# Two low parts per batch moved from GpSimd to VectorE in a decoder layer's cross-attention

## The reference

```python
x = x + attn(layernorm(x))                       # one head of 128, 256 keys
x = x + cross_attn(layernorm(x), ctx_768)        # 16 heads of 64, 1601 keys of width 96
x = x + ffn(layernorm(x))                        # router picks 31 rows a batch; attention
                                                 # among them, then a GELU MLP; others pass through
# the cross-attention, per head:
sim  = (x @ Wq)_h @ (context @ Wk)_h.T * 64 ** -0.5
out  = softmax(sim) @ (context @ Wv)_h ;  y = concat(out) @ Wo + bo
```

## Time and profile before

| | |
|---|---|
| median of 3 runs | 2159.55 us (2159.05 to 2160.88) |
| the profiled execution, its own time | 2161.14 us |
| its span, first to last instruction | 2159.90 us |
| granted TensorE clock over the span | 0.997 |
| busy: PE, DVE, ACT, POOL | 2078.4, 1723.5, 1796.4, 1936.6 us |

### The profile page before, as it was taken

The page is one execution under the profiler, slowest core; times in us unless marked ns, Lnnn a source line. Parts: engine busy times, 40 slices in busy tenths (PEclk is TensorE's granted clock), DMA queues, the critical chain, the costliest instruction groups (busy, mean ns, idle before and its releaser), DMA issues.

```text
span 2159.9 us, 57506 instructions
## 1 busy us (share of the span) xinstructions
PE 2078.4 (96%) x21697; PEld 1409.5 (65%) x21697; DVE 1723.5 (80%) x4158; ACT 1796.4 (83%) x3064; POOL 1936.6 (90%) x1129
## 2 busy tenths in 40 slices
PE   8999999999999999999999999999999999999998
PEld 4667666666766666666666666667666666666664
DVE  7778878787887878879687787887878788886864
ACT  5888898888888888898788888888888888888872
POOL 3899999999999899999899998998999999899991
PEclk9999999999999999999999999999999999999999
DMA  3211000010100001010010100101000010100000
GB/s 75 59 38 30 2 16 16 2 29 2 30 2 10 21 2 29 2 30 2 11 29 2 30 2 2 29 2 29 2 19 21 2 29 2 17 2 2 2 11 11
DMA packets 70483, 35.16 MB, mean 16 GB/s; under 512 B 58944, under 2 KB 68032, under 8 KB 70208
## 3 DMA queue, kind: packets, MB, share of 16 engines
q1 hardware_dynamic: 69104, 31.28, 6.2%
q10 hardware_dynamic: 1104, 0.20, 0.1%
HBM read 16.46 MB, written 2.10 MB: 9 GB/s over the span
## 4 chain that ended last, share of the span: by engine, by line
PE 73%; DVE 13%; issue 6%; ACT 5%; POOL 2%; DMA 0%; DVEq 0%; SPq 0%; ACTq 0%; POOLq 0%
PE PS L585 13%; PE PS L626 13%; PE PS L586 13%; PE PS L602 11%; PE PS L604 10%; DVE EH L1102 5%; PE PS L649 4%; PE PS L636 2%; DVE over L1128 2%; PE PS L659 2%; ACT PF L910 2%; POOL EL L1580 2%; ACT EH L917 1%; ACT over L932 1%; DVE junk L1373 1%
## 5 line engine op out<-in xcount | busy, mean ns | idle before, releaser
L1580 POOL TENSOR_TENSOR EL<-PF,EH 128x1024 f16<-128x1024 f32 x828 | 1761.7, 2154 | 132.6 <-DVE EH L1102 60.7
L910 ACT ACTIVATE PF<-PS 128x512 f32<-128x512 f32 x1664 | 973.4, 600 | 218.8 <-PE PS L586 203.2
L602 PE MATMUL PS<-Ch,EH 128*128 128x97 f16 (+1 forms) x6656 | 762.2, 207 | 35.6 <-POOL EL L1580 32.0
L602 PEld LDWEIGHTS PS<-Ch,EH 128*128 128x128 f16 (+1 forms) x6656 | 604.3, 97 | 283.2 <-issue 109.4
L1102 DVE TENSOR_SCALAR_CACHE_REDUCE EH<-PF 128x1024 f16<-128x1024 f32 x621 | 746.0, 1209 | 17.6 <-ACT PF L910 17.6
L604 PE MATMUL PS<-Cl,EL 128*128 128x97 f16 (+1 forms) x6656 | 758.9, 206 | 0.0
L1128 DVE CUSTOM_DVE_ANT_1 over<-over,PS 128x802 f32<-128x802 f32 x512 | 505.1, 987 | 289.7 <-PE PS L626 146.5
L604 PEld LDWEIGHTS PS<-Cl,EL 128*128 128x128 f16 (+1 forms) x6656 | 594.6, 98 | 155.0 <-issue 1.4
L585 PE MATMUL PS<-AH,ChT 98*128 98x512 f16 x1664 | 635.2, 382 | 8.9 <-ACT PF L910 6.2
L586 PE MATMUL PS<-AL,ClT 96*128 96x512 f16 x1664 | 632.9, 380 | 0.0
L932 ACT ACTIVATE over<-PS 128x802 f32<-128x802 f32 x512 | 431.3, 842 | 32.7 <-PE PS L626 12.3
(11 more groups left out here) (250 smaller groups left out, 1653.4 us busy)
## 6 DMA issues: line engine op xcount, KB each, us to landing
Cf<-in_ctx SPq DMA_DIRECT2D x16, 576.0 KB
X<-in_x SPq DMA_DIRECT2D x16, 128.0 KB, 2.5
out_x<-X SPq DMA_DIRECT2D x16, 128.0 KB, 1.7
msk<-in_attention_mask SPq DMA_DIRECT2D x4, 256.0 KB, 4.5
AH<-mh SPq DMA_DIRECT2D x63, 2.0 KB
xWqT<-in_xWqT SPq DMA_DIRECT2D x2, 256.0 KB, 5.9
xWo<-in_xWo SPq DMA_DIRECT2D x2, 256.0 KB, 3.8
fw<-in_fw SPq DMA_DIRECT2D x2, 256.0 KB, 3.1
```

The costliest lines, as they stand in the source:

```text
L602: pe.matmul(PS[:, 6, u0:u0 + DC + 1], EH[0:kr, r, qs], Ch[j][0:kr, t, 0:DC + 1], start=(t == 0 and q == 0), stop=False, skip_group_check=True)
L910: act.activation(PF[:, n % PRING, :], PS[0:KP, 4 + n % 2, :], ACT.Exp).then_inc(sg("ex"), 1)
L1580: pool.tensor_tensor(EL[:, r - 1:r + 1, :], PF[:, f - 1:f + 1, :], EH[:, r - 1:r + 1, :], ALU.subtract).then_inc(sg("lo_pool"), 1)
```

## The change

Pairs 8 and 36 of each batch (tiles 16 and 17, 72 and 73) get their low part from VectorE and not from GpSimd. For both, the high part is ScalarE's. The place in the order stays: VectorE makes it right behind its rounding of pair 9 or 37. Since the low parts of a batch now count on two semaphores in another pattern, `lowered` looks the counts up in two tables. `LAST_PAIRS` is 828, the first of the last four pairs.

```diff
--- before.py
+++ after.py
@@ -45,6 +45,7 @@
 AV_LAG = 8
 ROUND_LAG = 2
 LO_LAG = 4
+LOW_BY_DVE = (8, 36)
 NQ = 4
 NKEY = -(-NC // NQ)
 EARLY = 4
@@ -480,9 +481,18 @@
                 return sg("eh_act"), p - LAST_PAIRS + LAST_PAIRS // 4 + 1
             return (sg("eh_act"), p // 4 + 1) if p % 4 == 0 else (sg("eh_dve"), p // 4 * 3 + p % 4)
 
+        LOW_PAIRS = TILES // 2
+        def low_by_dve(p):
+
+            return p >= LAST_PAIRS or p % LOW_PAIRS in LOW_BY_DVE
+
+        dve_lows = [p for p in range(TOTAL // 2) if low_by_dve(p)]
+        dve_low_at = {p: x + 1 for x, p in enumerate(dve_lows)}
+        pool_low_at = {p: x + 1 for x, p in enumerate([p for p in range(TOTAL // 2) if p not in dve_low_at])}
+
         def lowered(p):
 
-            return (sg("lo_dve"), p - LAST_PAIRS + 1) if p >= LAST_PAIRS else (sg("lo_pool"), p + 1)
+            return (sg("lo_dve"), dve_low_at[p]) if p in dve_low_at else (sg("lo_pool"), pool_low_at[p])
 
         def bank_of(s):
 
@@ -1101,7 +1111,7 @@
                         w.wait_ge(sg("av"), n - ERING + 1)
                     dve.tensor_scalar(EH[:, r - 1:r + 1, :], PF[:, f - 1:f + 1, :], KEEP, None, ALU.mult, ALU.add,
                                       accum_out=esum[:, r // 2:r // 2 + 1]).then_inc(sg("eh_dve"), 1)
-                elif k == "lo" and s.a[0] >= LAST_PAIRS:
+                elif k == "lo" and low_by_dve(s.a[0]):
                     n = 2 * s.a[0] + 1
                     f, r = n % PRING, n % ERING
                     w.wait_ge(sg("ex"), n + 1)
@@ -1568,7 +1578,7 @@
                     which = int(k[-1])
                     w.wait_ge(sg(f"ln_mv{which}"), i)
                     rsqrt(rstd[:, which, :], mv[:, which, :, 1], T, 1.0, LN_EPS, f"ln_rstd{which}")
-                elif k == "lo" and s.a[0] < LAST_PAIRS:
+                elif k == "lo" and not low_by_dve(s.a[0]):
                     n = 2 * s.a[0] + 1
                     f, r = n % PRING, n % ERING
                     w.wait_ge(sg("ex"), n + 1)
```

## The result

The changed kernel takes 2182.10 us (median of 4, 2181.46 to 2184.00), the kernel before 2159.49 on the same chip (median of 4, 2159.05 to 2160.88): a ratio of 1.0105 (95% interval 1.0088 to 1.0123). It is 22.6 us slower, where 8.1 us were forecast. The profiled execution took 2184.0 us with a span of 2182.7 at a granted clock of 0.998. Lines of the program behind the change stand 10 lower than before: 636 is now 646, 1102 is 1112, 1580 is 1590.

A forecast was written before the change was run, and what follows sets the result against it. TensorE (96% busy) sets the pace mostly, chained to VectorE and GpSimd in paced stretches. Terms 2.6 + 2.0 + 2.85 + 1.75 - 1.1 = +8.1 us on the 2159.55 median gave 2167.7; case range 2164 to 2174, 8 in 10 2158 to 2177.

The forecast's parts named there:

- The prices: Moved low part on VectorE: 1.2 us at pair 36, 1.5 to 1.6 at pair 8; keys' difference 1.5 instead of 0.57.
- The term of pair 14: Pair 8's move makes pair 14 0.3 us late in batches 1 to 4, 6, 8, 10, 12, 14: +2.6 us.
- the step that failed: Pair 36: work queued behind the low part up to 1.14 us late; TensorE loses at pair 43 or the spread keys.
- The three terms: Pair 36's move: pair 43 late, batches 0, 2, 3, +2.0 us; 6, 10, 14, +2.85; spread keys, 5, 9, 13, +1.75.
- moves with them: Batches 6, 10, 14: pairs 40 to 43 move by 0.93 us and TensorE, waiting at pair 43, too: +2.85 us.
- In 5, 7, 9, 11, 13 and 15 GpSimd waits before pair 12 or 13 anyway and the lateness is gone: Pair 8's move: in these batches GpSimd's waiting absorbs the lateness, so no loss is counted.
- In batch 0 TensorE comes later: Pair 8's move: in batch 0 TensorE comes later, so no loss is counted.
- The low part gets the lock when pair 35 ends: Batch 15, pair 36: VectorE goes first after GpSimd's pair 35; GpSimd loses 1.09 of 2.14 us saved: -1.1 us.
- No difference: Rival: lateness is won back at following TensorE waits; within 0.2%, some 4.3 us, 2163.1 us; chance 0.2.
- Faster: Rival: keys' difference gets in ahead of pair 10, pair 14 0.4 us earlier in up to 12 batches; 2153 us; chance 0.12.
- much slower: Rival: GpSimd wins at pair 36, TensorE 1.9 us late in 14 batches, +27 us, 2187 us; chance 0.08.
- the forecast 9.2 before batch 15: Sum of the loss terms for pairs 8 and 36, 2.6 + 2.0 + 2.85 + 1.75 us, without batch 15's -1.1.

The follow-up runs named there:

- experiment 3: Against only pair 36's low part moved to VectorE: that low part put behind the projection's sum, 2195.91 us; or the sum put one place earlier, 2171.98 us.
- Experiment 2: Kernel before, no low part moved, plus a 1.22 us VectorE instruction with one SBUF input at pair 36's place: 2176.36 us, ratio 1.0070.
- experiment 5: Only pair 8 on VectorE, keys' difference two places later in VectorE's order: 2154.60 us; that shift alone in the kernel before: 2158.38 us.
- pair 28: Only pair 28's low part moved to VectorE, against the kernel before: 2148.45 us, ratio 0.9950.
- low part of pair 32: Only pair 32's low part moved to VectorE, against the kernel before: 2177.09 us, ratio 1.0093.
- the filler: Only pair 32's low part on VectorE, with an added VectorE instruction of some 0.7 us ahead of it: 2176.35 us, ratio 1.0076 against the kernel before.

## Why the prediction was wrong

**What held.** The work ends up slower by waits of VectorE's making; GpSimd's relief goes into its idle time (102.8 us waiting for roundings, 60.7 before), and the 1.98 us before pair 14 are still 1.98. GpSimd and TensorE at pair 14 of batch 3, with the earlier trace rows before:

```profile
473.19 4.23 POOL L1590 TENSOR_TENSOR EL<-PF,EH 128x1024 f16<-128x1024 f32 x2 [1.98 <-DVE EH L1112]
...
475.47 0.20 PE L612 MATMUL PS<-Ch,EH 128*128 128x97 f16 x1 [0.41 <-POOL EL L1590]
```

The prices held: 1.22 us at pair 36 (batches 0 to 14), 1.62 to 1.66 at pair 8 (forecast 1.5 to 1.6), line 1131 at a median of 1.535 (forecast 1.5). The term of pair 14, 9 x 0.29 = 2.6 us, was 2.9, though part of it shows at pair 10 already. One sign failed: GpSimd's busy time was to fall by about 64 us and fell by 42.8, because its low parts behind the moved ones carry their wait for VectorE as busy time. And one reading was slightly off: 469.02 less 468.88 is 0.14 and not 0.12, which changes no term. The trace agrees with the Trainium skill's page "SBUF — State Buffer", section "Who interferes with whom", that VectorE's two-input instructions and GpSimd's exclude each other.

**Pair 36, the step that failed.** "All that is queued behind it is late by up to 1.14: the projection's sum, the rounding of pair 38, a maximum, the queries' low part" is what happened. But I followed that lateness only through the roundings, to GpSimd and pair 43, and never asked who waits for the sum. TensorE does, 0.6 us later in the same place. Forecast for the place: +4.85 us at pair 43 and 1.75 at the spread keys; measured: 14.7 at pair 36, in all batches but the last, and nothing at pair 43, since TensorE then arrives there later itself. The three terms were real mechanisms hidden below a larger one, as experiment 3 shows; two had about the forecast size at their pair, but only 0.45 to 0.49 of 0.67 and 0.4 of 0.95 were kept, so "moves with them" held for less than half of that 0.95. The third has its size as a wait (0.60 against 0.58), to which TensorE's clock adds 1.7 to 3.4 us when the wait is that long. Experiment 2 shows the 1.03 to be a matter of the queue alone.

**Pair 8, "In 5, 7, 9, 11, 13 and 15 GpSimd waits before pair 12 or 13 anyway and the lateness is gone".** This again follows GpSimd only. The keys' difference, forecast rightly to be 1.0 late, has VX or XA right behind it in those five batches, and TensorE's projection waits for them: 4.8 us. "In batch 0 TensorE comes later" was wrong too: the rounding of pair 9 makes TensorE wait 0.41 us more at pair 8 (the same in experiment 5), and the clock fell behind it for 1.55, which may be chance. Together 6.8 us where 0 stood.

**Batch 15, "The low part gets the lock when pair 35 ends", -1.1 us.** VectorE did not get it. Its low part there took 4.85 us, behind a normalization and pair 37 of GpSimd:

```profile
2105.74 4.85 DVE L1120 TENSOR_TENSOR EL<-PF,EH 128x1024 f16<-128x1024 f32 x1
```

TensorE lost 1.1 us at pair 36 and had 0.7 back at pair 37. The table's -0.8 for that batch is what is left of this loss, less the fall of the clock that only the execution before had there.

**The rivals.** "No difference" assumed that lateness is won back; in batches 0 to 14 TensorE won back none of what it lost at pairs 9 and 36. "Faster" and "much slower" both exist, 0.4 us at pair 14 and 1.9 at pair 36, one step of VectorE's order away from the change; in the change itself neither happened. The sum of the terms seen at their places, 14.7 + 4.8 + 2.9 + 2.0 = 24.4 us, takes the place of the forecast 9.2 before batch 15.

## What to carry to other kernels

When work is put into an engine's queue, go through every instruction that is queued behind it up to that engine's next idle time, and for each ask who waits for it: also for the small ones that only free a PSUM bank. An average load says nothing here: GpSimd was at 90% and VectorE at 80%, and the same 1.22 us in VectorE's queue cost 1.0 us a batch at pair 36 and gained 0.9 at pair 28. And of two engines that exclude each other, an instruction that now meets the other is longer itself and makes all behind it late; put it where nothing urgent is behind it, as the keys' difference in experiment 5.

## What the runs showed of the hardware

A VectorE instruction with two SBUF inputs that waits for the shared port isn't always next when GpSimd's instruction ends. If GpSimd's following instruction is ready, either may go first, and a lost meeting costs one more GpSimd instruction, 2.1 us:

| GpSimd in a low part, its next one a low part | VectorE asked before GpSimd's end, us | the next one's rounding was ready before that end, us | lost |
|---|---|---|---|
| low part of pair 8, five kernels | 0.54 to 0.58 | 0.46 to 0.51 | 0 of 75 |
| first half of a split, batches 5 to 14, 14 kernels | 0.86 to 0.88 | 0.79 to 0.80 | 0 of 140 |
| the same, batches 1 to 4 | 0.95 to 1.00 | 0.87 to 0.92 | 11 of 56 |
| low part of pair 32, batches 1 to 14 | 1.14 to 1.17 | 1.07 to 1.10 | 12 of 14 |
| the same with the filler ahead of it | 0.54 to 0.55 | 1.07 to 1.10 | 9 of 14 |

The Trainium skill ("SBUF — State Buffer", "Who interferes with whom") says that issue order decides who blocks. By that VectorE, which asked 0.5 to 1.2 us before GpSimd could have started its next instruction, would win all five; the trace agrees for the first two rows, nearly always for the third, and disagrees for the others.

What decides stays open. It isn't the time that VectorE has asked, since 0.54 never lost in the first row and lost nine times in the last. The third column orders the rows: the longer GpSimd's next low part had been ready, the more meetings VectorE lost, and the filler, which did not change that time, helped little. This was read from the traces only; no run changed that time alone. It can't be the whole rule either: the second halves of 185 splits, asked 0.75 us before the end of a low part with a normalization next that had been ready for 1.9 us, all went first.

The other surprise is the clock. A wait of TensorE of 1.81 to 1.84 us for the spread keys was followed by a granted clock of 0.50 in five of six cases (batches 5, 9 and 13 in both kernels of experiment 3), one of 1.21 to 1.24 us at the same place in before and after in none; but a wait of 1.48 us in batch 0 was followed by it in two of the 14 kernels, and a wait of 1.76 us between pairs 43 and 44 of batches 7 and 11 in 23 of 28 cases. So 0.6 us more of waiting cost up to 3.7 us, and executions of one kernel differ too: the granted clock of the 23 of the kernel before lies between 0.996 and 0.999, where one fall (1.7 us) takes 0.0008. What decides between a fall and none for the same wait is open.
